# Straight-line strips for three engines and a second patch buffer in a deformable-convolution kernel

## The reference

```python
om = conv3x3_same(align, om_w, om_b)                    # offsets and mask logits
off, mask = om[..., :n_off], sigmoid(om[..., n_off:])   # 8 groups x 9 taps
# dcn_v2: each pixel, group and tap reads coarse_up (the 32x32 map resized to 64x64)
# at its own place, bilinearly, times its mask; then
out = einsum('bhwkc,kcf->bhwf', val, weight) + bias     # 9 taps x 256 -> 256
return x + relu(out) + fine_cal                         # inside the kernel's last stage
```

## Time and profile before

| | us |
|---|---|
| median of 3 runs | 3370.52 (3359.72 to 3374.48) |
| the profiled execution, own time | 3370.08 |
| its span, first to last instruction | 3368.4 |
| PE busy | 3117.9 (93% of the span) |
| DVE busy | 2515.5 (75%) |
| ACT busy | 1517.4 (45%) |

### The profile page before, as it was taken

The page is one execution under the profiler, slowest core; times in us unless marked ns, Lnnn a source line. Parts: engine busy times, 40 slices in busy tenths (PEclk is TensorE's granted clock), DMA queues, the critical chain, the costliest instruction groups (busy, mean ns, idle before and its releaser), DMA issues.

```text
span 3368.4 us, 91473 instructions
## 1 busy us (share of the span) xinstructions
PE 3117.9 (93%) x34242; PEld 2697.5 (80%) x34242; DVE 2515.5 (75%) x4215; ACT 1517.4 (45%) x2787; POOL 335.5 (10%) x445
## 2 busy tenths in 40 slices
PE   8969999999999938999998999998999998999999
PEld 7859999989999827878776777777777786877788
DVE  3427888888888859878776877887787786878782
ACT  0012222222222116656655565665666565656663
POOL 2000000000000001111111111111111111111111
PEclk9979999999999969999999999999999999999999
DMA  5322344333333232322223222223222233322222
GB/s 165 100 88 73 58 69 71 60 47 52 61 58 55 30 60 43 62 58 61 55 62 58 60 54 64 63 53 68 53 60 54 61 65 55 64 55 61 54 62 57
DMA packets 452882, 211.30 MB, mean 63 GB/s; under 512 B 230821, under 2 KB 447541, under 8 KB 452277
## 3 DMA queue, kind: packets, MB, share of 16 engines
q1 hardware_dynamic: 426112, 161.74, 26.6%
q10 hardware_dynamic: 21724, 26.37, 2.4%
q0 software_dynamic: 4608, 16.78, 1.3%
HBM read 104.86 MB, written 55.23 MB: 48 GB/s over the span
## 4 chain that ended last, share of the span: by engine, by line
PE 48%; ACT 7%; issue 6%; DVE 2%; ACTq 1%; SPq 1%; DMA 0%; POOL 0%; DVEq 0%; POOLq 0%
PE eb L1555 26%; PE tb L1113 14%; PE vb L1135 6%; ACT taps_all L1084 2%; ACT res L1142 1%; ACT wtT L1118 1%; ACT om L1040 1%; PE eb L1148 1%; PE tb L1035 1%; ACTq L1006 1%; DVE wt L1107 1%; ACT mask L1049 1%; ACT ot L1153 0%; SPq L1030 0%; ACTq L1435 0%
## 5 line engine op out<-in xcount | busy, mean ns | idle before, releaser
L1555 PE MATMUL eb<-val,wd 128*128 128x256 f32 (+1 forms) x4680 | 1225.7, 385 | 0.0
L1118 ACT COPY wtT<-tb 128x512 f32<-128x512 f32 x1152 | 662.7, 587 | 682.2 <-PE tb L1113 680.8
L1555 PEld LDWEIGHTS eb<-val,wd 128*128 128x128 f32 x4680 | 798.4, 191 | 120.8 <-issue 57.4
L1113 PE MATMUL tb<-ident,wt 128*128 128x128 f32 x4608 | 710.2, 278 | 85.7 <-issue 37.0
L1113 PEld LDWEIGHTS tb<-ident,wt 128*128 128x128 f32 x4608 | 564.7, 143 | 239.6 <-issue 77.1
L1107 DVE TENSOR_TENSOR wt<-taps_all 128x768 f32<-128x768 f32 x768 | 731.4, 994 | 10.4 <-PE tb L1113 2.1
L547 PE MATMUL conv<-fine,wf 128*108 128x256 f32 x4608 | 593.5, 290 | 13.1 <-DVE omT L878 13.1
L547 PEld LDWEIGHTS conv<-fine,wf 128*108 128x108 f32 x4608 | 572.8, 174 | 28.7 <-issue 28.7
L1488 DVE COPY val<-vb 128x432 f32<-128x432 f32 (+1 forms) x384 | 212.7, 554 | 240.4 <-PE vb L1135 240.1
L1135 PE MATMUL vb<-wtT,win 64*32 64x144 f32 x16384 | 323.3, 292 | 60.7 <-issue 56.4
L1135 PEld LDWEIGHTS vb<-wtT,win 64*32 64x32 f32 x16384 | 245.6, 108 | 108.5 <-issue 108.0
(11 more groups left out here) (142 smaller groups left out, 2499.8 us busy)
## 6 DMA issues: line engine op xcount, KB each, us to landing
val<-val SPq DMA_DIRECT2D x128, 396.0 KB, 3.8
win<-cpad SPq DMA_DIRECT2D x304, 64.0 KB
om_s<-om_d SPq DMA_DIRECT2D x1152, 12.0 KB
chunk<-in_x SPq DMA_DIRECT2D x32, 512.0 KB, 5.0
xchunk<-in_x SPq DMA_DIRECT2D x32, 512.0 KB, 4.1
r_d<-r POOLq DMA_DIRECT2D x32, 512.0 KB, 3.2
rt<-r_d SPq DMA_DIRECT2D x63, 256.0 KB, 4.9
out<-ot ACTq DMA_DIRECT2D x63, 256.0 KB, 2.9
```

What stands on the lines that cost most here:

```text
L1113: last = nc.tensor.transpose(tb[b][:, 128 * j:128 * j + 128], wt[half][:, 4 * i + j, :], ident[:])
L1118: return nc.scalar.copy(dst, src) if e == "act" else nc.vector.tensor_copy(dst, src)
L1555: done = nc.tensor.matmul(eb[q][:, 256 * fo:256 * fo + rows], wd[:, half, k, 128 * fo:128 * fo + 128], val[:, half, k, at:at + rows // W, ...
```

## The change

`loop` no longer has a hardware loop: the code of all 34 double strips is written out for PE, ACT and DVE, with constants in place of registers. `win` has a second buffer; image b uses buffer b % 2. SP loads all 16 transfers of an image's first window in one go (`whole_windows`), signalled by `win_whole`: for image 0 ahead of its strips, for image b + 1 ahead of strip 12 of image b. What that load waits for is the end of sampling of image b - 1 at the latest. The first strip of an image has no window transfers of its own. PE waits for both `win_whole` and `win_ready` ahead of the first runs. SP's program is written out by image, with a loop over two groups of four strips inside; POOL's loops stay.

```diff
             def loop(e, strips):
-                strips(0)
-                strips(1)
-                with e.Fori(2, ST // 2 - 1) as it:
-                    strips(it)
-                for it in range(ST // 2 - 1, ST // 2 + 2):
+                for it in range(ST // 2 + 2):
                     strips(it)
...
+                def whole_windows(b):
+
+                    w(sp, "sampled", 6 * SI * (b - 1))
+                    windows(b, b * (PADC * PADC * C), range(WIN), sems["win_whole"])
+
                 def strip(b, i, turn):
...
                     w(sp, "sampled", 6 * s)
-                    if turn is None:
-                        windows(at, range(2, WIN), sems["win_first"])
-                        h(sp, "win_first", 16 * 12 * (b + 1))
-                        windows(at, range(0, 2), sems["win_ready"])
-                    else:
-                        at = at + 2 * (i - turn) * (PADC * C)
+                    if turn is not None:
+                        at = b * (PADC * PADC * C) + 2 * (i - turn) * (PADC * C)
...
-                        windows(at, range(2 * turn + 6, 2 * turn + 8), sems["win_ready"])
+                        windows(b, at, range(2 * turn + 6, 2 * turn + 8), sems["win_ready"])
...
-                opening(0)
-                with sp.Fori(1, 4) as m:
-                    four(0, 4 * m)
-                with sp.Fori(1, B - 1) as b:
-                    opening(b)
-                    with sp.Fori(1, 4) as m:
-                        four(b, 4 * m)
-                opening(B - 1)
-                with sp.Fori(1, 3) as m:
-                    four(B - 1, 4 * m)
-                four(B - 1, 12)
+                whole_windows(0)
+                for b in range(B):
+                    opening(b)
+                    with sp.Fori(1, 3) as m:
+                        four(b, 4 * m)
+                    if b + 1 < B:
+                        whole_windows(b + 1)
+                    four(b, 12)
...
                     if known(s, 0, ST):
                         n = 2 * s + hx
-                        copied, loaded, kept = (v if isinstance(v, int) else pe.to_reg(v) for v in (
-                            batch_no(s, hx, NT - 1) + 1, 64 * (s + 1), 3 * n))
-                        pe.wait_ge(consts, CONSTS)
-                        w(pe, "tb_out", copied)
+                        w(pe, "tb_out", batch_no(s, hx, NT - 1) + 1)
                         if hx == 0:
-                            w(pe, "win_ready", loaded)
-                        w(pe, "kept_near", kept)
-                        w(pe, "kept_far", kept)
+                            w(pe, "win_whole", 16 * 16 * (s // SI + 1))
+                            w(pe, "win_ready", 64 * (s // SI * (SI - 1) + s % SI))
+                        w(pe, "kept_near", 3 * n)
+                        w(pe, "kept_far", 3 * n)
```

More of the change, by code:

```diff
@@ L958, in sample_and_project @@
         NSUM = NK * 256
-        win_all = sb("win", [128, 2 * BLK * 128])
-        win = win_all[:].rearrange("p (j c) -> p j c", c=128)
+        win_both = [sb(f"win{i}", [128, 2 * BLK * 128]) for i in range(2)]
+        wins = [t[:].rearrange("p (j c) -> p j c", c=128) for t in win_both]
+        win_all, win = win_both[0], wins[0]
         VROWS, VCOLS = 12, W + 2
@@ L1125, in bank_of, with sample_blocks @@
             return vb[u][v % 2][:, 0:NK * 4 * m].rearrange("p (k y x) -> p k y x", k=NK, y=4)
-        def sample_blocks(half, v, window):
+        def sample_blocks(half, v, window, win):
             for j in range(*THIRDS[v]):
@@ L1159, in fast @@
             names = ("om_loaded masked pchain coef_ready dist_ready achain capped products batched tb_out based "
-                     "win_first win_ready sampled kept_near kept_far cleared sides entered crossed ready projected finished "
+                     "win_whole win_ready sampled kept_near kept_far cleared sides entered crossed ready projected finished "
                      "r_ready summed turned ob_out out_stored duplicated").split()
@@ L1220, in duplicate_rows, with windows @@
                                      ).then_inc(sems["duplicated"], 16)
-                def windows(at, rows, signal):
+                def windows(b, at, rows, signal):
                     for a in rows:
@@ L1227, in windows @@
                                           ap=[[C, WIN], [2 * C, 2 * BLK], [1, 128]])
-                            sp.dma_start(win[part:part + WIN], src).then_inc(signal, 16)
+                            sp.dma_start(wins[b % 2][part:part + WIN], src).then_inc(signal, 16)
+                def whole_windows(b):
+                    w(sp, "sampled", 6 * SI * (b - 1))
+                    windows(b, b * (PADC * PADC * C), range(WIN), sems["win_whole"])
                 def strip(b, i, turn):
@@ L1233, in strip @@
                     p = 0 if turn is None else turn % 2
-                    at = b * (PADC * PADC * C)
                     w(sp, "sampled", 6 * s)
-                    if turn is None:
-                        windows(at, range(2, WIN), sems["win_first"])
-                        h(sp, "win_first", 16 * 12 * (b + 1))
-                        windows(at, range(0, 2), sems["win_ready"])
-                    else:
-                        at = at + 2 * (i - turn) * (PADC * C)
+                    if turn is not None:
+                        at = b * (PADC * PADC * C) + 2 * (i - turn) * (PADC * C)
                         if not isinstance(at, int):
                             at = sp.snap(at)
-                        windows(at, range(2 * turn + 6, 2 * turn + 8), sems["win_ready"])
+                        windows(b, at, range(2 * turn + 6, 2 * turn + 8), sems["win_ready"])
                     if known(s - 2, 0, ST):
@@ L1568, in first_runs @@
                         n = 2 * s + hx
-                        copied, loaded, kept = (v if isinstance(v, int) else pe.to_reg(v) for v in (
-                            batch_no(s, hx, NT - 1) + 1, 64 * (s + 1), 3 * n))
-                        pe.wait_ge(consts, CONSTS)
-                        w(pe, "tb_out", copied)
+                        w(pe, "tb_out", batch_no(s, hx, NT - 1) + 1)
                         if hx == 0:
-                            w(pe, "win_ready", loaded)
-                        w(pe, "kept_near", kept)
-                        w(pe, "kept_far", kept)
+                            w(pe, "win_whole", 16 * 16 * (s // SI + 1))
+                            w(pe, "win_ready", 64 * (s // SI * (SI - 1) + s % SI))
+                        w(pe, "kept_near", 3 * n)
+                        w(pe, "kept_far", 3 * n)
                         for v in range(2):
-                            sample_blocks(hx, v, lambda j: BLK * hx + j).then_inc(sems["sampled"], 1)
+                            sample_blocks(hx, v, lambda j: BLK * hx + j, wins[s // SI % 2]).then_inc(sems["sampled"], 1)
                 def third_run(s, p, hx):
@@ L1587, in third_run @@
                         w(pe, "kept_far", one)
-                        sample_blocks(hx, 2, lambda j: BLK * hx + j).then_inc(sems["sampled"], 1)
+                        sample_blocks(hx, 2, lambda j: BLK * hx + j, wins[s // SI % 2]).then_inc(sems["sampled"], 1)
                 def slot(t, p, hx):
@@ L1735, in pe_general @@
                                     hold(pe, sems["added"], 6 * t + 2)
-                                sample_blocks(0, v, lambda j: 0).then_inc(sems["sampled"], 1)
+                                sample_blocks(0, v, lambda j: 0, win).then_inc(sems["sampled"], 1)
                             w(pe, "added", 6 * (t + 1))
```

## The result

The changed kernel runs in 3241.28 us (median of 4 runs, 3238.97 to 3242.82), against 3369.99 us before in the same comparison. The ratio is 0.9622, with a 95% interval of 0.9599 to 0.9645. The profiled execution took 3242.4 us with a span of 3240.7; forecast were 3245.1 for it and 3225 to 3290 for the range.

A forecast was written before the change was run, and what follows sets the result against it. PE was taken to bound undisturbed strips at 30.37 us. 3370.1 - 138.5 (excess) + 1.5 (start stays) + 4 (late edges) + 8 (strip 12) = 3245.1 us; range 3225 to 3290.

The forecast's parts named there:

- What bounds the kernel: Whole strip pipeline: PE bounds an undisturbed strip at 30.37 us; only the 138.5 us above that pace can go.
- Part 1, the amount: Starts of loop passes 2 to 29: writing the loop out removes 28 x 3.40 = 95.1 us.
- Part 1, the cause: Starts of loop passes: the jump back causes all of the 3.40 us each, and goes when written out.
- Constants give nothing: Written-out strips: constants in place of registers keep the loop's pace, 30.42 and 30.35 us against 30.37.
- Late edges, 4 us: PE's sampling runs in written-out code: instruction packets arriving late at their edges cost 4.4 us, taken as 4.
- upper bound of 42 us, with its rival: PE's sampling runs: late edges cost at most 42 us; rival of late edges in nearly every strip, 3283 us, 12%.
- Part 2, 39 us out: Three changes of image: with the first window in place beforehand, PE's waits of 39.0 us go.
- Strip 12, 8 us: Strip 12 of an image: urgent windows queue behind 16 transfers, costing 2.7 us each, 8 us for three changes.
- supply too slow: Packet edges on PE: instructions can't be fetched fast enough over straight code, 372 us more, 3613 us; 4%.
- DVE as the bound: Strips without pauses of PE: DVE's chain with ACT sets 31 us a strip, 3281 us; 3%.
- The wait that moves to strip 12: Strip 12: the queue is full and each change of image still costs about 13 us, 3276 us; 5%.
- The jumps weren't the cause of issue: Starts of loop passes: jumps didn't cause PE's late instructions and 34 us intervals stay, 3339 us; 1%.

The follow-up runs named there:

- the two free paddings: The kernel before, loops and windows kept, with 64 or 128 idle instructions ahead of PE's strips: 3275.48 and 3279.21 us.
- loops_only: The kernel before with the strips of PE, ACT and DVE written out, one window buffer kept: 3278.69 us, ratio 0.9744.
- pe_only: The kernel before with PE's strips alone written out, ACT and DVE keeping their hardware loop: 3280.77 us, ratio 0.9745.
- window_only: The changed kernel's two window buffers and SP program, but with hardware loops on PE, ACT and DVE, one per image: 3270.82 us, ratio 0.9718.
- shifted: The changed kernel with 128 already met waits (64 instructions) put ahead of PE's strips: 3239.59 us.
- the second profile: The changed kernel run once more, unchanged, to compare the places of its gaps: 3242.72 us.
- behind_wait: The changed kernel with the next first window's 16 transfers moved behind strip 12's wait for `sampled`: 3285.66 us, ratio 0.9752.
- pad64: The kernel before, loops and windows kept, with 128 already met waits (64 instructions) ahead of PE's strips: 3275.48 us, ratio 0.9719.

## Why the prediction was right, and where its reasons were not

**What bounds the kernel**: right. Strips at the undisturbed pace with PE busy throughout, and a sum of what lies above them, gave the time to 3 us of the profiled execution. No other engine came up behind: DVE still waits 2.6 us a strip for ACT, as in the earlier trace rows.

**Part 1, the amount**: right, 95.1 us forecast. The two kernels with PE written out and the old windows, and the two free paddings, give 84 to 93. `loops_only` spends 3 us of it on strips of 30.42 us, `pe_only` 8 on strips of 30.50.

**Part 1, the cause**: wrong. The step that failed is "All that is caused by the jump, and the jump goes". What goes is the refetch of the body. A jump whose body is still on the chip takes no time that the marks show (30.38 us across it), and the kernel before could have had the gain with its loop in place. The trace before had the hint: 346 packets of instructions (on its page), 36 of them in four passes, where I looked only at the stretch of written-out strips and took it that the number of fetched instructions doesn't change. It does, from 346 to 279. The sum was right since writing out removes the refetch at the jump whatever its cause; but a forecast for another loop on the ground of "3.4 us a jump" would have been wrong, as the one for `window_only` was, by 37 us. The size isn't luck, since it was read from the trace of this very placement; that there was anything to gain is, for with 64 idle instructions ahead the kernel before runs in 3275 us, and writing the loop out would then have gained nothing.

**Constants give nothing**: right, a little less than nothing, 0.05 us a strip. This 3 us stood in no term.

**Late edges, 4 us**: 0.44 + 1.10 us of gaps inside runs in the profiled execution, 0.9 and 0.8 in the two others, 2.3 in `loops_only`. Oversized; that they are edges of packets is supported, not shown. The 13 packets that the term started from were PE's alone, not those of all engines, and the passes without a gap are 26 of 29, not 25. The upper bound of 42 us, with its rival, was too wide: `shifted` has one gap.

**Part 2, 39 us out**: right; 37 to 41 by `loops_only` against the changed kernel.

**Strip 12, 8 us**: oversized. The step was 17.2 us for 16 transfers at 61 GB/s. SP's queue moved 108 GB/s in image 0 of the profiled execution (0.97 MB from 1617 to 1626) and nearer 80 at strip 44 (0.94 MB from 2590 to 2602), and PE waited 0, 0 and 1.15 us; in the second profile 1.61 at strip 12 and 1.55 at strip 44. A single row of rate, from a stretch in which PE came to stand, carried this term; the lower bound of 0 was the better value. The rate is no accident, for it is there again in `behind_wait` (64 GB/s from 1625 to 1638, 0.83 MB), but it isn't the rate of this place, and no run shows why. `behind_wait` shows that the danger was real and what it costs when it comes: 44 us.

**What moved the total back**: the marks gave 7.4 us less than forecast, but the first mark came 3.8 us later (1295.81 against the earlier trace rows) and the end 0.9 later, which no term had. Of the 3.8, 2.1 us had already arisen in the last row of PE in the stage before (1204.03 and 1206.17). 3245.1 - 7.4 + 3.8 + 0.9 = 3242.4.

**The rivals**: supply too slow and DVE as the bound are out by the strips of 30.42 us. The wait that moves to strip 12 is what `behind_wait` makes of it. "The jumps weren't the cause of issue" got 1%, with the condition that the long intervals stay. They didn't; yet its first half came nearer to the cause than the forecast did.

## What to carry to other kernels

When an engine comes late to the first instructions of a pass, compare the packets of its instruction queue per pass with those of one copy of the body: refetching is the cost, and writing the loop out or a few instructions ahead of it removed it here; a shorter body wasn't tried. Moving code is the cheapest thing to try, and also the control without which a gain by unrolling can't be explained; the idle instructions must fit into time in which the engine waits. A bulk load belongs ahead of a wait that its queue would stand in anyway; the same load behind that wait cost as much as the one it replaced.

## What the runs showed of the hardware

- PE ran passes of two strips, about 6.6 packets of 16 KB, without fetching a single packet, from 1480 to 3100 in `pad64`. With the same body placed otherwise it fetched 9 packets each pass and lost 3.4 us. Writing out made it 29 packets in 260 us, at 0.05 us a strip: fetching is not dear, fetching after a jump is. The Trainium skill (Runtime: NRT & Kernel Launch, Instruction fetch mechanics) has a taken branch stall when its target isn't in the current two pages. It names blocks of 16 KiB and, for PE, 128 KiB in all: two such blocks can't hold this body, so the free passes contradict a window of that size; the 128 KiB can, and agree. The prediction had left out the condition on the target.
- With one placement out of four (192 instructions) it varied from pass to pass whether packets were fetched (six of 28 jumps), and the time spread by 24 us between runs.
- Window transfers of 64 KB ran at 61 GB/s at the first change of image before and at 64 in `behind_wait`, while SP's queue moved 108 GB/s ahead of strip 12 after, at a DMA share of 0.59, 0.64 and 0.67. The cause wasn't looked for.
